# Projections as products of fp16 halves, softmax sums from a column of ones, no filler products, and the second expert product two chunks behind the first

## The reference

```python
h = h @ A + gu_t                                  # scan over rows and columns, both directions
y = (yr + yc) * 0.25
out0 = g * y + (1.0 - g) * x                      # layer 0
...
q, k, v = x @ Wq + bq, x @ Wk + bk, x @ Wv + bv   # layer 1, on the layer norm of out0
o = softmax(q @ k.T / sqrt(32), over the window) @ v
x1 = x + o @ Wo + bo
...
p = softmax(x @ gate_w + gate_b)                  # on the layer norm of x1; best two of four experts
y = gelu(x @ w1 + b1) @ w2 + b2                   # 192 -> 768 -> 192
out = x1 + sum of p * y over the two
```

## Time and profile before

| | before |
|---|---|
| median of three runs | 3214.75 us (3212.38 to 3215.9) |
| the profiled execution | 3210.95 us |
| its span in the profile | 3209.2 us |
| mean granted clock of TensorE | 0.92 |
| busy: PE / DVE / ACT / POOL | 2742.2 / 1883.9 / 1060.5 / 906.1 us |
| one image of 2 to 14, from attention to attention | 180.1 to 183.1 us |
| of this, attention | 46.1 us |
| from the last attention's end to the end (experts of image 15 and the last pass) | 254.6 us |

### The profile page before, as it was taken

The page is one execution under the profiler, slowest core; times in us unless marked ns, Lnnn a source line. Parts: engine busy times, 40 slices in busy tenths (PEclk is TensorE's granted clock), DMA queues, the critical chain, the costliest instruction groups (busy, mean ns, idle before and its releaser), DMA issues. The chain is left out here.

```text
span 3209.2 us, 50697 instructions
## 1 busy us (share of the span) xinstructions
PE 2742.2 (85%) x18097; PEld 2020.8 (63%) x18097; DVE 1883.9 (59%) x5344; ACT 1060.5 (33%) x3333; POOL 906.1 (28%) x672
## 2 busy tenths in 40 slices
PE   0478888998898999988998999998898989999597
PEld 0356575766667676666666676766667666766364
DVE  4454555666666566666656566566656566565464
ACT  0032423234242424334242424334242424334122
POOL 0001203050422415050422415050422415050544
PEclk9787978899998989999999989899998999899799
DMA  3430103132242415132242415133232415133564
GB/s 40 95 103 15 56 15 97 35 83 57 74 92 59 104 56 111 36 79 61 73 89 63 104 55 110 32 83 63 72 89 61 107 52 109 36 83 70 136 158 99
DMA packets 272634, 241.80 MB, mean 75 GB/s; under 512 B 209020, under 2 KB 250494, under 8 KB 261760
## 3 DMA queue, kind: packets, MB, share of 16 engines
q1 hardware_dynamic: 211648, 147.17, 17.9%
q0 software_dynamic: 50880, 52.59, 9.7%
q10 hardware_dynamic: 9856, 38.80, 3.8%
HBM read 133.29 MB, written 73.59 MB: 64 GB/s over the span
## 5 line engine op out<-in xcount | busy, mean ns | idle before, releaser
L1504 PE MATMUL PSUM<-XT,WB 128*128 128x512 f16 x2010 | 528.2, 396 | 24.5 <-DMA META<-slots 24.5
L795 ACT ACTIVATE HF<-PSUM,WB 128x512 f32<-128x512 f32 x402 | 275.8, 686 | 799.5 <-PE PSUM L1504 796.5
L1522 PE MATMUL PSUM<-WB,HHI 128*128 128x192 f16 x1608 | 404.2, 251 | 75.6 <-DVE HLO L1043 74.3
L818 ACT ACTIVATE PSPT<-PSUM,NMX 94x126 f32<-94x126 f32 x1056 | 366.9, 358 | 307.7 <-PE PSUM L1563 250.2
L1040 DVE TENSOR_SCALAR HHI<-HF 128x512 f16<-128x512 f32 x402 | 180.7, 450 | 407.3 <-ACT HF L795 404.2
L693 POOL DMA_INDIRECT out_dram<-Y,META x228 | 359.4, 1576 | 200.9 <-DVE Y L1068 117.6
L1524 PE MATMUL PSUM<-WB,HLO 128*128 128x192 f16 x1608 | 404.3, 251 | 0.0
L1523 PE MATMUL PSUM<-WB,HHI 128*128 128x192 f16 x1608 | 404.3, 251 | 0.0
L1504 PEld LDWEIGHTS PSUM<-XT,WB 128*128 128x128 f16 x2010 | 199.3, 103 | 197.6 <-issue 37.6
L1551 PE MATMUL PSUM<-KBD,QT 128*94 128x378 f32 x704 | 291.0, 495 | 18.8 <-ACT PSPT L818 17.2
L1043 DVE SCALAR_TENSOR_TENSOR HLO<-HF,HHI 128x512 f16<-128x512 f32 x402 | 282.6, 703 | 13.8
(11 more groups left out here) (269 smaller groups left out, 4978.5 us busy)
## 6 DMA issues: line engine op xcount, KB each, us to landing
WB<-weights SPq DMA_DIRECT2D x67, 1600.0 KB, 7.0
XR<-in_x ACTq DMA_DIRECT2D x16, 768.0 KB, 5.8
out_dram<-X ACTq DMA_DIRECT2D x32, 384.0 KB, 2.4
weights<-WB ACTq DMA_DIRECT2D x4, 1600.0 KB, 6.4
GUP<-TGU SPq DMA_DIRECT2D x256, 8.0 KB, 1.8
slots<-XROW,IDX POOLq DMA_INDIRECT x256, 2.4
out_dram<-Y,META POOLq DMA_INDIRECT x228, 3.6
HF<-in_w ACTq DMA_DIRECT2D x6, 384.0 KB, 4.6
```

Source lines behind the costliest of these rows:

```text
L795: act.activation(HF[:, k % 2, :], PSUM[:, 4 + k % 2, :], ACT.Gelu, scale=1 / (X_UP * W_UP), bias=bias).then_inc(f["gelu_done"], 1)
L818: e = act.activation(PS[0:QS, n % 2, h, :], PSUM[0:QS, n % 2, h * KS:(h + 1) * KS], ACT.Exp, bias=NMX[:, b, n % 2, h:h + 1], accum_out=DEN ...
L1504: mm = pe.matmul(dst, WB[:, ws, w:w + 128], XT[:, xs, chunk, :], start=(n == 0), stop=(n == 4))
L1522: pe.matmul(dst, HHI[:, k % 2, tok], w2h, start=False, stop=False, skip_group_check=True)
```

## The change

Four things change.

1. **Projections.** XN is scaled and split on DVE into XNR, a high and a low fp16 half side by side (384 columns), in two steps of four token tiles (new L1049, L1050). PE transposes XNR in three chunks of 128 (24 fp16 transposes for 16 fp32 ones), the windows hold three chunks (ACT copies two of them, DVE one), and each product of a piece is five fp16 matmuls over 128 rows (`X_CHUNK`) in place of two fp32 ones over 96. The weights are split once at the start. The evacuations scale the result back. XNR lies in X2's memory and waits for X2 to be free.
2. **Sums of the softmax.** V gets a column of ones per head (`VC = HD + 1`), so that the product with V also gives the sum. The accumulator reads on ACT go; DVE takes the reciprocal from PSUM behind the product, and copies one row of the sums (DEN).
3. **No filler products** in attention (those in the first `conv` stay).
4. **Order of the experts.** `ffn2` of a chunk runs two chunks behind `ffn1`; HHI and HLO have three buffers; `block_out` comes at the third chunk of the next block, and the waits of `STEPS` and the empty steps are set anew.

```diff
-                for t in range(4 * k, 4 * k + 4):
-                        for j in range(2):
-                            mm = pe.transpose(PSUM[0:HC, 2 * j + t // 4, (t % 4) * 128:(t % 4 + 1) * 128],
-                                              XN[:, t, j * HC:(j + 1) * HC], EYE[:])
+                        for c in range(3):
+                            mm = pe.transpose(PSUMH[:, c * T + t * 128:c * T + (t + 1) * 128],
+                                              XNR[:, t, c * 128:(c + 1) * 128], EYEH[:])
...
-                    for j in range(2):
-                        mm = pe.matmul(PSUM[0:HC, n % 4, 0:width], W[:, j, oh * HC:(oh + 1) * HC],
-                                       XW[:, j, b0:b1, keys], start=(j == 0), stop=(j == 1))
+                    for m, c in enumerate(X_CHUNK):
+                        mm = pe.matmul(PSUM[0:HC, n % 4, 0:width], WQKV[:, kind, m, oh * HC:(oh + 1) * HC],
+                                       XW[:, c, b0:b1, keys], start=(m == 0), stop=(m == 4))
...
+                for k in range(2):
+                    tiles = slice(4 * k, 4 * k + 4)
+                    dve.wait_ge(s["xn1_ready"], at("xn1_ready", i, k + 1))
+                    link(dve.tensor_scalar(XNR[:, tiles, 0:C], XN[:, tiles, 0:C], X_UP, None, ALU.mult))
+                    dve.scalar_tensor_tensor(XNR[:, tiles, C:2 * C], XN[:, tiles, 0:C], X_UP, XNR[:, tiles, 0:C],
+                                             ALU.mult, ALU.subtract).then_inc(s["xnr_ready"], 1)
+                    yield
...
-                                               ACT.Exp, bias=NMX[:, b, n % 2, h:h + 1],
-                                               accum_out=DEN[:, b, n % 2, h:h + 1])
+                                               ACT.Exp, bias=NMX[:, b, n % 2, h:h + 1])
...
-                    dve.wait_ge(s["exp_done"], at("exp_done", i, 2 * b + 2))
-                    link(dve.reciprocal(RDEN[:, b, :, :], DEN[:, b, :, :]))
                     dve.wait_ge(s["pv_done"], at("pv_done", i, b + 1))
+                    o = PSUM[0:QS, 2, O_COL:O_COL + HEADS * VC].rearrange("p (h d) -> p h d", h=HEADS)
+                    dve.tensor_copy(DEN[:, b, :, :].rearrange("p a h -> p (a h)"), o[0:1, :, HD])
+                    link(dve.reciprocal(RDEN[:, b, :, :].rearrange("p a h -> p (a h)"), o[:, :, HD]))
...
-                        keep_busy(8 if b == 1 else 2)
...
-                    if n > 1 and k == 1 and j:
-                        block_out(i, j - 1)
                     if k == 2:
+                        if j:
+                            block_out(i, j - 1)
                         block_gates(i, j)
...
-                    if n >= 1:
-                        ffn2(i, *divmod(n - 1, HK))
+                    if n >= 2:
+                        ffn2(i, *divmod(n - 2, HK))
```

More of the change, by code:

```diff
@@ L30 @@
 QS = QB + 1
+VC = HD + 1
 E, HID = 4, 768
@@ L461, in hybrid_kernel, with windows @@
         STEPS_AHEAD = 1
-        STEPS = [(1, 1) if n < 16 else (2, 1) if n < 20 else (2, 2) for n in range(NSEL * HK)] + [(1, 1)]
-        def windows(copy, j, part, give):
+        STEPS = [(1, 1) if n < 16 else (2, 1) if n < 18 else (2, 2) for n in range(NSEL * HK)] + [(1, 1)]
+        def windows(copy, c, part):
             if part == 0:
-                copy(XW[0:HC, j, 1:NB - 1, 0:KW],
-                     window_view(PSUM, j * T + QB - PAD + 1, [HC, [QB, NB - 2], [1, KW]]))
-                return
-            copy(XW[0:HC, j, 0, PAD - 1:KW], window_view(PSUM, j * T, [HC, [1, KW - PAD + 1]]))
-            last = (NB - 1) * QB - PAD + 1
-            copy(XW[0:HC, j, NB - 1, 0:T - last], window_view(PSUM, j * T + last, [HC, [1, T - last]]))
-            copy(XW[0:HC, j, :, KW], window_view(PSUM, j * T, [HC, [0, NB]])).then_inc(give, 1)
+                return copy(XW[:, c, 1:NB - 1, 0:KW],
+                            window_view(PSUMH, c * T + QB - PAD + 1, [128, [QB, NB - 2], [1, KW]]))
+            copy(XW[:, c, 0, PAD - 1:KW], window_view(PSUMH, c * T, [128, [1, KW - PAD + 1]]))
+            copy(XW[:, c, NB - 1, 0:T - LAST_KEY], window_view(PSUMH, c * T + LAST_KEY, [128, [1, T - LAST_KEY]]))
+            return copy(XW[:, c, :, KW], window_view(PSUMH, c * T, [128, [0, NB]]))
+        LAST_KEY = (NB - 1) * QB - PAD + 1
+        UNSCALE = 1 / (X_UP * W_UP)
+        X_CHUNK = (0, 0, 1, 2, 1)
         SPANS = [(0, 4), (4, 8), (8, NB)]
@@ L776, in conv @@
                     yield
-                yield from empty(2)
-                act.wait_ge(s["xn1T_done"], at("xn1T_done", i, 1))
-                windows(act.copy, 0, 0, s["win_act"])
-                yield
-                windows(act.copy, 0, 1, s["win_act"])
-                yield
+                yield from empty(4)
+                act.wait_ge(s["xn1T_done"], at("xn1T_done", i, 1))
+                windows(act.copy, 0, 0)
+                windows(act.copy, 0, 1)
+                yield
+                windows(act.copy, 2, 0)
+                windows(act.copy, 2, 1).then_inc(s["win_act"], 1)
+                yield
+                yield from empty(2)
                 for n in range(PIECES):
@@ L1022, in conv @@
                         yield
-                yield from empty(6)
+                yield from empty(3)
+                for half in range(2):
+                    dve.wait_ge(s[X2_FREE[half]], at(X2_FREE[half], i, 1))
+                for k in range(2):
[4 more added lines that the diff above has]
+                                             ALU.mult, ALU.subtract).then_inc(s["xnr_ready"], 1)
+                    yield
+                yield from empty(3)
                 dve.wait_ge(s["xn1T_done"], at("xn1T_done", i, 1))
-                windows(dve.tensor_copy, 1, 0, s["win_dve"])
+                dve.memset(XW[:, :, 0, 0:PAD - 1], 0.0)
+                dve.memset(XW[:, :, NB - 1, T - LAST_KEY:KW], 0.0)
+                windows(dve.tensor_copy, 1, 0)
                 yield
-                windows(dve.tensor_copy, 1, 1, s["win_dve"])
+                windows(dve.tensor_copy, 1, 1).then_inc(s["win_dve"], 1)
                 yield
+                yield from empty(2)
                 for n in range(PIECES):
@@ L1202, in gates @@
                 dve.wait_ge(s["route_exp"], at("route_exp", i, 0))
+                if not (isinstance(i, int) and i == B):
+                    dve.wait_ge(s["mixed"], at("mixed", i, 1))
                 link(dve.tensor_reduce(sm1, se, AX.X, ALU.add))
@@ L1448, in conv @@
                         yield
-                yield from empty(4)
+                yield from empty(6)
                 pe.wait_ge(s["mixed"], at("mixed", i, NT))
@@ L1462, in conv @@
                     yield
-                yield from empty(3)
+                yield from empty(4)
                 pe.wait_ge(s["win_act"], at("win_act", i, 1))
@@ L1693, in experts @@
                 chunks = blocks_of(i) * HK
-                for n in range(chunks + 1):
-                    a, b = STEPS[n % len(STEPS)] if n < chunks else (1, 1)
+                for n in range(chunks + 2):
+                    a, b = STEPS[n % len(STEPS)] if n < chunks else (0, 0)
                     if n < chunks:
```

116 lines of the change are left out of this document (67 added, 49 removed).

## The result

The changed kernel takes 3387.07 us (median of 4 runs, 3377.22 to 3394.76) beside 3213.57 us before: a ratio of 1.054, interval 1.0509 to 1.057. It is 173 us slower; 36 us faster were forecast, and the time lies outside the stated range of 3130 to 3205 us and the wider one of 3100 to 3290.

A forecast was written before the change was run, and what follows sets the result against it. PE is nearly always busy, paced by a PE-DVE loop in attention and mostly streaming in the expert stage. -1.65 us an image (-21 over thirteen periods), -8 for images 0 and 1, -6 for the last pass: 3179 us, range 3130 to 3205.

The forecast's parts named there:

- Projections: First Q product to first score: five fp16 products replace fp32 ones, 24.06 us to 15.2, a gain of 8.9 us an image.
- Windows: Ahead of the first projection: XNR on DVE and a third chunk of copies delay it 1.0 us, bounds 0 and 3.
- The waits: Expert stage: the 5.5 us of split waits can go, but three other waits make the third tile's mix 3.3 us late.
- The scan: Expert stage: PE waits at the scan, whose input needs 16 GUP moves issued by SP; near 3 us.
- the tokens: Before the router: normalisation starts near 1728 and PE waits for the normalised activations, some 5 us.
- Y: Block 1's Y stands on DVE behind the gate operations, so PE waits 4.1 us instead of 0.98.
- (a): Expert stage: the scan's input is made about 1.4 us earlier, so the scan ends about 3.2 us earlier.
- the later block 0: Block 0's last second product comes at 1714.2, 2.5 us later, delaying SP's weight load and the state moves behind it.
- The clock: Falls at attention's end, after Y and at the transposes, about 0.3 to 0.6 us each; 1.3 us an image.
- Rival A: Clock falls inside attention without the dummies, an image gets 3 to 6 us longer, 3250 to 3290 us; chance 0.26.
- rival B: Attention stays at 1.2 GHz for half its blocks or more, +208 us, 3390 us and up; chance 0.07.
- Attention: Later reciprocal and copy cost 1.35 + 0.6, dropped dummies and ACT reads save 0.6 and 0.4: +1.0 us, bounds -1 and +2.

The follow-up runs named there:

- run 1: Changed kernel, but ACT issues the load of the next image right behind the layer norm, not at the start of attention; 3279.19 us, ratio 1.0201.
- run 9: Changed kernel with the second expert product one chunk behind and the early load of the next image, without fillers; 3107.91 us, ratio 0.9685.
- run 14: Kernel before with only the second expert product two chunks behind (three buffers for the halves, memory shared to make room); 3404.26 us, ratio 1.057.
- run 10: run 5 with the softmax sums from ACT's accumulator again and the reciprocal ahead of the products with V; 3085.89 us, ratio 0.9606.
- run 5: Changed kernel with the second expert product one chunk behind, the early load of the next image and the fillers back; 3107.36 us, ratio 0.9681.
- run 15: Changed kernel with one chunk behind, fillers and sums from ACT, the load left where it was; 3184.57 us, ratio 0.9907.
- run 3: Changed kernel with the second expert product one chunk behind the first again, nothing else; 3233.53 us, ratio 1.0042.
- run 4: Changed kernel, but SP issues the next image's state moves ahead of the load of the third block's weights; 3259.53 us, ratio 1.0142.
- run 13: Changed kernel with one chunk behind (two in the last pass), early load, state moves first, sums from ACT, no fillers; 3058.82 us, ratio 0.9523.

## Why the prediction was wrong, point by point

In the forecast's own terms, the profiles of the two kernels give this for an image (us, mean of images 2 to 14; attention goes from its first score product to the end of its last product with V):

| stretch | before | changed | forecast | measured |
|---|---|---|---|---|
| attention | 46.1 | 52.4 | +1.0 | +6.3 |
| from there to the first projection (windows, waits, clock) | 101.7 | 117.3 | +5.6 | +15.7 |
| from there to the next attention (projections, end of the image) | 33.3 | 25.5 | -8.25 | -7.9 |
| whole period | 181.1 | 195.2 | -1.65 | +14.1 |

So the gain came nearly as forecast, and the loss was forecast far too small in two places: the wait for the input load in attention, which no term had, and the expert stage, which costs nearly three times its price; runs 1, 9 and 14 put that down to the order of the experts. Outside these periods, images 0 and 1 were to give 8 us and cost 3.5 (up to the attention of image 2), and the last pass was to give 6 us and gave 2. (The 254.6 us of the table before end with PE's last product; to the end of the execution it is 271.7 us before and 269.7 in the changed kernel.)

The runs divide the loss by the edits. Projections, with the load issued early: run 10 against the kernel before, 127 us less. Column of ones: 21 more (run 5 against run 10). Fillers: 1 more without them (run 9 against run 5), which is nothing. Order: 171 more (run 1 against run 9). These four are one chain of runs up to run 1. The load where it was: 99 more in the old order (run 15 against run 10) and 108 more in the new one (the changed kernel against run 1). With the 99 the sum is 165 us; 173 were measured. So the effects add up to within some 9 us; the size of each depends on the order of the steps by as much and more: the new order costs 154 us beside the late load (the changed kernel against run 3) and 190 in the kernel before (run 14).

- **Projections, the net right, in part by luck.** 8.9 us an image less 1.0 for the windows, 7.9, were worked out, and 127/16 is 7.9. But by the distances between starts, without the expert chunks between them, the projections of image 8 take 24.1 us before and 16.0 after: 8.1 less, not 8.9. And the rest of the period is hardly longer: in run 10 the period of images 2 to 14 is 8.2 us shorter than before. Two small misses cancel. That run 10 also issues the load early should matter little: in the kernel before, DVE waits for the load once, in image 0, for 5.5 us. The price taken for V's products, 0.0825 us each, is the one measured. Fifteen of them, each with its own weights of 126 columns, stand at

```profile
1909.22 1.40 PE L1525 MATMUL PSUM<-WQKV,OSX 128*126 128x192 f16 x15
```

  with starts 0.0825 us apart, as the second products have, whose weights have 128 columns.
- **Windows, not singled out.** In image 8 it is 9.9 us from the first transpose to the first projection and was 8.9, the 1.0 us of the sum. But other pieces stand in that stretch as well, and in run 10 it is 7.1 us, with the same windows and the old order.
- **The waits, right; what they hold up, wrong.** The scan (3.7 for "near 3"), the tokens (6.6 for 5), Y (3.7 for 4.1) came as foretold. The step that failed is (a), "The scan then ends about 3.2 us earlier": it ends 36.9 us behind attention where it ended at 35.3. The GUP moves start at 18.4 us behind attention, 16.3 before, and not 1.4 earlier. The products that their input is made from (L1373 before, L1408 after) stand behind the second first product and ahead of the first second product in both kernels, so no second product stood ahead of them that could move; and PE's clock was at 0.50 from 1763.0 to 1773.2, where it came out of attention. The 3.2 us that were to pay for the later block 0 did not exist. From the scan's end to block 0's last product I had 10.7 us; image 3 shows that number, image 8 14.6, with the clock at 0.50 in 11.5 us of that stretch. So block 0 ends 51.4 us behind attention in place of 40.0, where 2 to 3 us later were forecast.
- **The clock, wrong in size.** I took 1.3 us an image, by a price of 1.4 us for 3.6 us lost (0.2 us for each us at a clock of 0.50; the prediction writes 1.2 GHz, the profile gives the share alone). That price came from the earlier trace rows, from an order in which a slow PE eats into waits. In the changed kernel the five matmuls of a first product (L1539) stand 2.14 us from their start to that of the next product at 0.50 (1768.55 to 1770.69) and 1.08 us at 1.00 (1774.54 to 1775.62). In the new order PE's own products release the chain (the weight load on SP waits for a second product), and slow time counts nearly in full: image 8 has 13.7 us more at 0.50 than image 3 and its period is 6.6 us longer, 0.48 us for each. There is also far more of it. Image 8 before is at 0.50 twice, 13.7 us around the scan and 3.4 at the transposes. In the changed kernel it is so six times, 58 us in all: 6.8 us behind the stall in attention, 10.2 at attention's end, 20.5 around the scan, 6.8 behind the wait for the tokens, 6.8 behind that for Y and 6.8 at the transposes. The prediction had the end of attention, Y and the transposes. That the slow time causes the longer period, and not the waits that it follows, is argued from these rows; no run holds the clock and leaves the waits.
- **The input load, missing.** No term, no rival and no row had it. In the kernel before, the load that belongs to image 9's attention is issued 1.4 us ahead of it (1804.24), takes 5.8 us, and the first statistics on it come 8 us into that attention (1813.63): a slack of 3.6 us. The projections are 8 us shorter, so the next attention starts, and the load is issued, among other transfers. In image 8 of the changed kernel it is issued at 1712.37; the two weight loads of 1600 KB are issued at 1704.42 and 1712.25 and take 7.7 and 11.3 us to landing, the first transpose is issued at 1713.37, and the scatter of the outputs (out_dram, L711) goes on from 1702.32 to 1721.5. The load then takes 12 us. The slack could have been read from the trace before, though not from the rows that the prediction had.
- **Rival A, half right.** The clock fell in every attention (0.81 to 0.93 in images 1 to 14) and the price was near (6.3 us for 3 to 6), but chiefly not for want of fillers. The stall was the larger cause: without it and without fillers attention has 0.94 to 0.99 (run 1). The measured 3387 us lies beside rival B's 3390, which is chance: in no image was attention at 0.50 for half its blocks (its lowest mean clock is 0.81, image 1). That a fall would last so long was my estimate, with no row behind it; run 13, without fillers, has attention of image 8 at 0.99.
- **Attention, right but for the load.** Without the stall attention takes 47.8 us in the new order (run 1) and 46.3 in the old one (run 9), on the mean of images 2 to 14: +1.7 and +0.2, inside the bounds of -1 and +2. The column of ones was put at 1.35 + 0.6 - 0.4 for itself; by run 10 it costs 1.3 an image, of which only half lies in attention.

## What to carry to other kernels

When a stage gets shorter, list every transfer that was hidden beside it or behind it and ask where it goes; the load that the waits of the kernel before don't show is one to check: here it had 3.6 us of slack. When an operation moves back in an order, follow every queue that waits for it, and price a wait on PE above its length: here 6 us of waiting came with 10 us an image (run 4). Where such a wait comes from a queue that merely happens to hold two things in a row, try the swap in that queue first: here it alone gave 128 us (run 4), where taking back the whole order gave 154 (run 3).

## What the runs showed of the hardware

- A load of 768 KB that took 5.8 us from issue to landing (median of the kernel before) took 12.0, 13.2 and 12.9 us (medians of the changed kernel, runs 3 and 15) where two weight loads are issued in the 8.0 us ahead of it and the first token transpose at most 1.0 us behind it (loads at 1712.37, 1819.88 and 1790.31), and 5.4 when issued 39 us ahead of attention (run 1, image 8: 1796.0 and 1835.4) and not 0.8.
- Taking away a wait of 6 us of PE gave 10 us an image (run 4); the clock of the stretch around it went from 0.81 to 0.86 with it (image 8).
- Attention without fillers, PE busy 38.0 of 46.0 us, is at 0.99 of the clock (run 13, image 8). In the changed kernel PE idles for 5.1 us up to 1727.0 in attention, and the clock is at 0.50 from 1725.4 to 1732.3.
- fp16 products of 192 columns, each with its own weights of 126 columns, start every 0.0825 us (changed kernel, L1525).
